# The query-key products of an audio transformer block as three fp32r products of 128 columns each, in place of one fp32 matmul per head

## What is computed

```python
h = tok(x, W, b)                                  # path signatures to depth 4, times W, 128 features
h = h + attn(layernorm(h), w_qkv, ..., w_out)     # 8 heads of 64, softmax over a sequence
h = h + ffn(layernorm(h), gate_w, w1, w2, w3, sw1, sw2)   # 8 experts, top 1, and a shared gelu network

# in attn, per head:
dots = einsum('bhid,bhjd->bhij', q, k) * exp(temperature)
out  = einsum('bhij,bhjd->bhid', softmax(mask(dots)), v)
```

## Time and profile before

| | |
|---|---|
| median of three runs | 715.73 us |
| the profiled execution's own time | 715.07 us |
| its span (first to last instruction) | 713.1 us |
| TensorE matmul busy | 664.4 us, 93% of the span |
| TensorE weight loads busy (beside the matmuls) | 512.9 us, 72% |
| VectorE, ScalarE, GpSimd busy | 436.7, 297.4, 334.1 us |
| mean granted TensorE clock | 0.977 |

### The profile page before, as it was taken

One profiled execution on the slowest core, in us unless ns is written; L12 is line 12 of the kernel. 1 busy time (PEld: TensorE's weight loads), 2 busy tenths in 40 slices (PEclk: granted clock), 3 DMA queues, 4 the chain that ended last, 5 costly groups with the idle time before them and its releaser, 6 DMA issues.

```text
span 713.1 us, 13737 instructions
## 1 busy us (share of the span) xinstructions
PE 664.4 (93%) x3976; PEld 512.9 (72%) x3977; DVE 436.7 (61%) x1085; ACT 297.4 (42%) x701; POOL 334.1 (47%) x344
## 2 busy tenths in 40 slices
PE   4789999999999999999999999998879769999993
PEld 1567777777778777877777777876769737777772
DVE  6676776767766776767676776765374125445441
ACT  3314444454435444454435444443746124434440
POOL 5765453454435453455445443541027704544553
PEclk9799999999999999999999999999899979999998
DMA  8915221112211211112111211121244222323230
GB/s 329 171 64 203 49 47 33 37 34 61 63 37 33 58 37 37 33 44 52 33 37 33 63 33 37 33 56 41 66 173 136 75 56 40 42 39 41 38 41 5
DMA packets 40847, 45.28 MB, mean 63 GB/s; under 512 B 6272, under 2 KB 29184, under 8 KB 40448
## 3 DMA queue, kind: packets, MB, share of 16 engines
q1 hardware_dynamic: 34192, 40.86, 21.5%
q0 software_dynamic: 6640, 4.22, 4.3%
HBM read 17.30 MB, written 11.44 MB: 40 GB/s over the span
## 4 chain that ended last, share of the span: by engine, by line
PE 79%; POOL 8%; DVE 5%; issue 5%; DMA 1%; ACT 1%; SPq 0%; POOLq 0%; DVEq 0%
PE bank L1112 69%; POOL sorted_rows L523 4%; PE bank L1375 3%; PE bank L1271 2%; PE bank L1159 2%; PE bank L1251 1%; POOL e L432 1%; POOL e3l L444 1%; PE bank L1358 1%; POOL g L440 1%; POOL z L449 1%; DMA sq<-square 0%; PE bank L1193 0%; PE bank L1202 0%; DVE h L744 0%
## 5 line engine op out<-in xcount | busy, mean ns | idle before, releaser
L1112 PE MATMUL bank<-whigh,uth 128*128 128x512 f32 x512 | 168.4, 410 | 0.8 <-DVE lowt L740 0.8
L449 POOL TENSOR_TENSOR z<-z 128x512 f32<-128x512 f32 x32 | 40.8, 1276 | 182.3 <-DVE z L824 182.3
L1112 PEld LDWEIGHTS bank<-whigh,uth 128*128 128x128 f32 x512 | 89.8, 190 | 40.6 <-issue 25.5
L1112 PE MATMUL bank<-whigh,utl 128*128 128x512 f32 x256 | 100.9, 394 | 0.0
L531 POOL DMA_INDIRECT out<-z,ids x39 | 60.8, 1558 | 73.3 <-ACT z L703 73.0
L458 POOL TENSOR_TENSOR rstd<-rstd,powers 128x1 f32<-128x1 f32 x64 | 35.3, 552 | 71.3 <-DVE rstd L841 49.8
L1112 PE MATMUL bank<-xT,qkw 128*128 128x128 f32 x512 | 64.0, 279 | 0.0
L1085 DVE COPY xvp<-bank 128x512 f32<-128x512 f32 x39 | 27.0, 692 | 60.0 <-PE bank L1375 60.0
L562 ACT CAST uth<-bank 128x512 fp32r<-128x512 f32 x32 | 18.8, 586 | 105.6 <-PE bank L1164 105.6
L1112 PEld LDWEIGHTS bank<-xT,qkw 128*128 128x128 f32 x512 | 61.3, 196 | 0.1
L1112 PEld LDWEIGHTS bank<-whigh,utl 128*128 128x128 f32 x256 | 48.3, 189 | 11.2
(11 more groups left out here) (206 smaller groups left out, 1481.0 us busy)
## 6 DMA issues: line engine op xcount, KB each, us to landing
xvp<-xvo SPq DMA_DIRECT2D x128, 128.0 KB, 2.3
w<-w_t SPq DMA_DIRECT2D x1, 4096.0 KB, 13.4
sorted_rows<-x SPq DMA_DIRECT2D x3, 838.5 KB, 14.7
prob<-sorted_rows SPq DMA_DIRECT2D x39, 64.5 KB, 1.8
w<-w_high SPq DMA_DIRECT2D x4, 512.0 KB, 5.4
x_columns<-x2t SPq DMA_DIRECT2D x32, 64.0 KB, 1.6
xg_in<-x_columns SPq DMA_DIRECT2D x8, 256.0 KB, 3.2
levels<-w_t SPq DMA_DIRECT2D x1, 2048.0 KB, 8.6
```

What stands on the lines that cost most here:

```text
L449: G.tensor_tensor(z4[:], z[:, 0:4, :], z[:, 4:8, :], ALU.add).then_inc(tree, 1)
L1112: return T.matmul(out_, lhsT, rhs, start=start, stop=stop)
```

## The change

`qkw` gets a second half for `lo` and the type fp32r. ScalarE's copy at L629 becomes a cast to `hi`; VectorE gets two new subtractions of 512 columns behind `features_lo(0)`; `norm_columns` waits for them. In the iteration each head is made by `three` with `xTh` and `xTl` in place of one matmul with `xT`, and the wait for `xT_lo` moves ahead of the heads. The lines of the changed kernel are five further down from L1112 on.

```diff
-        qkw = sb("qkw", [P, HEADS, DIM])
+        qkw = sb("qkw", [P, 2, HEADS, DIM], F32R)
...
+        qkw_lo = sem("query_key_weights_lo")
...
-                A.copy(qkw[:, 4 * n:4 * n + 4, :].rearrange("p h d -> p (h d)"), B[6 + n][:]).then_inc(qkw_sb, 1)
+                A.copy(qkw[:, 0, 4 * n:4 * n + 4, :].rearrange("p h d -> p (h d)"), B[6 + n][:]).then_inc(qkw_sb, 1)
...
             features_lo(0)
+            for n in range(2):
+                d.wait_ge(qkw_sb, n + 1)
+                lo, hi = (qkw[:, m, 4 * n:4 * n + 4, :].rearrange("p h d -> p (h d)") for m in (1, 0))
+                remainder(lo, B[6 + n][:], hi, qkw_lo)
             after(rest_made)
             add_s2(1)
...
-                pe.wait_ge(qkw_sb, 2)
+                pe.wait_ge(qkw_lo, 2)
...
                 if prev:
                     pe.wait_ge(vo_sb, 2 * i)
+                pe.wait_ge(xT_lo, i + 1)
                 for hd in range(HEADS):
                     by_head = B[5 + hd // 4][:].rearrange("p (s h k) -> p h s k", s=2, h=4)
-                    last = mm(by_head[:, hd % 4, :, :], qkw[:, place(hd), :], xT[:])
+                    last = three(by_head[:, hd % 4, :, :], [qkw[:, n, place(hd), :] for n in range(2)], x)
                     if hd % 4 == 3:
                         last.then_inc(g_psum, 1)
-                pe.wait_ge(xT_lo, i + 1)
```

## The result

The changed kernel takes 749.15 us (median of four runs: 745.66, 746.10, 752.20 and 752.32); the kernel before, run beside it on the same chip, 715.59 us. The ratio is **1.047 [1.041, 1.054]**: 33.6 us slower, where 27.9 were forecast. The predicted 743.6 us is 5.5 us short; the sign, the range and the main term hold. The profiled execution took 752.2 us, with a span of 750.2 us against 713.1.

A forecast was written before the change was run, and what follows sets the result against it. TensorE's own stream was taken to bound the tile loop. Tiles 0 to 29 +27.0, setup and waits 0, tile 31 +1 gave +27.9 us on the profiled 715.07, so 743.0, median 743.6 us; range 737 to 761.

The forecast's parts named there:

- The heads: Query-key products on TensorE: 24 loads at 0.112 us, 2.69 us against 1.79, so +0.90 us a tile.
- The bounds of 0.108 and 0.133: Low and high ends in us for a head product's spacing: +0.80 or +1.40 us a tile.
- How many tiles pay it: Tile loop: tiles 0 to 29 pay 0.90 us each, +27.0 us; tile 30 pays 0, covered by TensorE's softmax idle time.
- Tile 31: Last tile's heads, mostly at 1.2 GHz: +0.9 us if the clock rises as before, +1.7 if not; taken as +1.
- The waits for `xTl` and on `xqk`: Wait ahead of the heads, with 4.6 us to spare, and ScalarE's copies after them: 0 us.
- the levels: VectorE's setup levels begin 2.05 us late, at about 30.15, with the first still ready before TensorE needs it.
- The setup ... 0: VectorE's two new subtractions: their delay fits inside 3.14 us of VectorE idle time, 0 us; up to 2 without that cover.
- A: Rival for the heads: the stream sets the pace, 0.07 us a product, -3 to -5 us in all, 711 us; 6%.
- C: Rival for the heads: a short fp32r product costs more than its load; 801, 816 or 827 us; 7%.
- B: Rival for the heads: fp32r loads faster than the router's, 0.08 to 0.095 us a product, +5 us, 720 us; 3%.
- D: Rival for the heads: the repeated operand's second load is left out, 16 loads a tile as before, 716 us; 2%.
- Counting passes: Reading of the skill for the heads: three passes in place of four save 0.45 us a tile, some 14 us; not adopted.

The follow-up runs named there:

- moving_half: casts_ahead with 64 moving columns in each head product in place of 128; 739.52 us, one run.
- load_half: casts_ahead with 64 stationary columns in each head product in place of 128, all 128 moving ones kept; 711.44 us, one run.
- fp32_heads_sub: The kernel before, fp32 heads kept, with two added setup subtractions into an unused tile; 720.25 us against 715.24, ratio 1.0081.
- casts_ahead: The changed kernel with its two new subtractions moved behind the three small setup casts; 742.56 us against 715.24 for the kernel before, ratio 1.038.
- two_products: casts_ahead with two products a head, the one with the weights' low part left out; 738.27 us against 735.81 for the kernel before, ratio 1.0027.
- fp32_later_xn: The kernel before, fp32 heads kept, with only the transposes of `xn` moved behind one more chunk of the projection; ratio 1.0013.
- The bf16 kernel: casts_ahead with all three head products in bf16; ratio to the kernel before 0.9941, repeated at 710.24 us against 714.80, ratio 0.9944.

## Why the prediction was right, and where its sum was short

**"The heads": right.** Forecast 24 x 0.112 and +0.894 us a tile, measured 0.111 to 0.112 and +0.90. That the load is the cause was an inference from the router's 8-column products; the pair moving_half and load_half shows it on the heads themselves: half of the moving columns leaves 0.112, half of the stationary columns gives 0.060. The bounds of 0.108 and 0.133 were not needed. One sign was wrong: the fp32r records were to be shorter, 0.22 us, and are 0.27 to 0.28 us, as long as the fp32 ones. The record shortens with the stationary columns (0.22 us in load_half), not with the moving ones (0.28 in moving_half).

**"How many tiles pay it": right in sum.** Tiles 0 to 30 grew by 26.3 us in the trace, 27.0 were forecast (26.8 with the digits kept, so that the forecast's 27.9 should read 27.8). Tile 30 pays nothing, as said, but not for the reason given. The idle time ahead of `prob` has not shrunk: 1.76 us, after 1.77. VectorE takes up the softmax only 6.14 us after the start of the heads in both kernels, directly behind other work that goes back to GpSimd's `z` and not to the heads, and the transposes of `prob` start 9.95 us after it in both (498.41 - 488.46, 532.09 - 522.14). The later heads are absorbed further ahead. TensorE no longer waits 0.32 us for GpSimd's `z`: those products come 4.07 us after the start of the heads in place of 3.66, though the heads are 0.93 longer, and the rest goes in shorter gaps behind them. The missing 0.7 lies at the ends of the stage: tiles 0 and 1 pay 0.7 and 0.5, and tile 30 is 0.2 shorter than before, with a granted clock of 0.64 in place of 0.54 from the transposes of `prob` on.

**Tile 31: "+1", mis-sized.** The bound of "+1.7" for a clock that "stays low for all" is what came: 5.16 - 3.32 = +1.8. The clock stayed at half through the `vow` products as well, which took 543.57 - 541.03 = 2.5 us against 507.15 - 505.68 = 1.5. Together this is +2.9 of the 3.6 us found behind tile 31's start; 0.7 is spread over the rest and not traced. The term is also not stable from kernel to kernel: the profile of fp32_heads_sub doesn't have the fall at all. Whether it differs between runs of one kernel too, and makes their two groups (4.7 and 5.8 us apart), is not shown, but there is a hint: moving_half took 739.5 us, as the lower group of casts_ahead, and tile 31's 24 products take 529.38 - 526.69 = 2.69 us in its timeline, at full clock, where those of casts_ahead take 533.58 - 528.42 = 5.16. Whether the clock falls isn't something that I could read from rows of one execution.

**The waits for `xTl` and on `xqk`: right.** Neither shows in the traces. What I said of the levels also held: they ran 1.8 us late, 2.05 forecast.

**"The setup ... 0": this step failed.** It cost 5 to 7 us: +5.0 alone with the fp32 heads (fp32_heads_sub, where the tail gave some back), 6 to 7 between the change and casts_ahead, 7.2 in the profiled execution at tile 0's start. I moved the casts and `tokbout` by 2 us and kept their durations, and so counted a "3.14 us idle" VectorE as cover. Nor was "without that cover it would be up to 2 us" a bound, since it priced the delay and not what the delayed work would run beside. In the kernel before, both casts start (31.70 and 31.83) ahead of GpSimd's `e3l` at 31.93; 2 us later they meet 5.8 us of GpSimd instructions back to back. The sign was there in the earlier trace rows: `tokbout`, 128 x 128 elements, took 1.38 us, where 512 columns out of a bank take 0.68. It ended with GpSimd's `e3l`, and I passed over it.

The stall then sets off a second cost. From 38.62 (before) and 42.47 (now) for the matmuls of `u` the start moves by 3.9 us; the other 3.4 of the 7.2 come after it, in a stretch whose clock is 0.50 where it was 1.00, behind TensorE's 5.32 us of idle time (1.1 before).

The Trainium skill, "SBUF — State Buffer", Who interferes with whom, describes such a hold: VectorE and GpSimd share a port pair, which an instruction of VectorE needs in a 2-port mode, or with two inputs in SBUF beside a GpSimd one that reads SBUF; whichever of the two issues first has it for its whole instruction, and the other waits. The traces agree: 5.41 and 5.49 us for instructions that take 0.2 to 0.3 when GpSimd is idle, and no hold for those with one input in a bank (0.68). Which mode the casts were in, no trace says. The traces add one thing: the loser was held over two GpSimd instructions in a row (L476 and L499), not only to the end of the first.

**The rivals.** A (stream pace) and C (a price of its own) are both excluded by moving_half and load_half. B (a load faster than the router's) is excluded for full 4-byte weights: 0.111 to 0.112 in every kernel; bf16 loads are faster, 0.056 at most. D (the second load left out) is excluded by two_products, whose repeated operands cost 0.112 like the rest. Counting passes, by which a quarter of the heads would have gone, has the wrong sign here.

With the setup's 7.2 us in place of 0, 26.3 in place of 26.8 and 3.6 behind tile 31's start in place of 1, the sum is the 37.1 us of the profiled pair. The profiled execution took 752.2 us, 9.2 above the forecast's 743.0 for it; the median of 749.15 lies nearer the forecast because two of the four runs took 746 us, and that is luck. The range of 737 to 761 held since it was left wide for the spacing, which came as forecast; nothing in it stood for the setup.

Not tried: splitting a head's stationary operand in two halves of 64 columns with fp32r products, so that each load is half as long. At load_half's 0.060 us a product the 48 products would take 2.9 us a tile (an estimate), more than the 2.69 of 24 full ones.

## What to carry to other kernels

Before replacing one fp32 matmul by several faster products, look at how many moving columns each has: with 128 of them and full 128-column weights of four bytes, the load sets the price (0.112 us), three fp32r products cost 1.5 times the fp32 one, and weights of two bytes are what helped (bf16: 0.056 us). Idle time of VectorE covers a delay only if what is delayed meets the same neighbours: look at what GpSimd does at the new time, and at any instruction there that already takes several times its size. And when a saving in the bound engine's stream doesn't arrive whole, find who is late next: one chunk moved past the `xn` transposes turned 0.6% into 1.6%.

## What was unexpected of the hardware

- VectorE was held for 5.4 us by GpSimd, over two of its instructions, for a 0.22 us cast; also for a plain addition (5.49 us).
- After 5.32 us without work on TensorE, the granted clock was 0.50 for 10 us with TensorE busy for 9.4 of 10.3 us.
- Chips differ: the kernel before took 715 us on some and 736 on others. Tiles are the same there (14.52 us in fp32_later_xn), and what differs lies in the tail. The bf16 kernel ran on both kinds, its profiled executions taking 733.72 and 709.93 us. In the same stretch of its tail, windows view, TensorE is busy for 10.36 us on the first chip and for 23.54 us on the second, at a granted clock of 0.56 against 0.89; what holds the engines there was not traced:

```profile
546.00:577.00 31.00, 10.36 (x39) 8.02 (x39) 3.17 (x5) 6.88 (x14) 16.49 (x18) 0.56 0.18 56
...
546.00:577.00 31.00, 23.54 (x145) 19.58 (x144) 5.44 (x11) 7.58 (x15) 15.36 (x17) 0.89 0.27 79
```
